# Cross attention and feed forward on one core: rows by DMA in the head, another order for q's third pair, and M and G in halves

## Chip, cores, metric

The kernel runs on one core of one Trainium2 chip. The metric is device time in microseconds of one execution; 16 blocks of the batch are worked off on that core.

## What is computed

The input x is (16, 128, 1024) and ctx is of the same shape; the middle dimension is the channel dimension of the attention (DIM 128), n runs over 1024 tokens, and there are 8 heads of 64. The reference, cut:

```
q: layernorm(x) over its last axis;  k = v = ctx
qh, kh, vh = Wq q, Wk k, Wv v            # (8 heads, 64, 1024)
qh = softmax(qh, over the 64) / 8;  kh = softmax(kh, over the 1024 tokens)
context = kh vh^T;  out = context^T qh;  out = Wo out + bo
x2 = x + out / max(norm(out over channels), 1e-12) * g * sqrt(128)
w = (4 bit weights from qweight, low and high nibble, minus round(zeros / scales)) * scales
result = x2 + layernorm(x2) w + bias
```

## The kernel before

One block is one index of the batch. The code writes a software pipeline of iterations i = -1 to 17, each of eight steps j = 0 to 7: iteration i prepares block n = i + 1 (load, normalise, split in high and low parts), does the projections of block a = i, the attention output of block c = i - 1 and the feed forward of block f = i - 2. Iterations 3 to 14 (on ACT to 12) are a hardware loop, the others are written out. Each engine runs its own instruction list in the order of the code; semaphores tie them together. There is no scheduler.

Per block: `project_q(j)` makes 128 tokens of q for all heads (three float32r products of high and low parts, into ps_q); DVE's `shift_q` takes off the maximum, ACT exponentiates, DVE's `sum_q` sums, GpSimd's `scale_q` normalises a pair of steps (pairs p = 0 to 3 are steps 2p and 2p + 1), ACT's `high_q` and GpSimd's `low_q` split the pair into two float16 tiles, and SP sends both through a transposing DMA (`turn_q`). `project_k(b, j)` makes 128 channels of k for all tokens (ps_k), DVE's `max_k` and ACT's `exp_k` work on it, PE transposes the result and ACT moves it to k_t. Since the context is linear in v, v is never projected: M = ctx^T k_exp (`mix_m`, eight full float32 products of 512 columns into ps_m, one for each 128 tokens), ACT moves it to m_t, and G = M^T vo for each head (`mix_g`, vo = Wv^T Wo^T made once in the head) goes to ps_o[0]. DVE's `split_g` scales G by k's sums into float16 g_hi and g_lo, in four column groups fc, and `mix_out(h)` gives the output for half h of the tokens, over the same four groups. ACT's `squares`, PE's column sums, GpSimd's rn and PE's spreads of rn give the norm; DVE's `attend` multiplies with it, GpSimd adds x_res to x2 and takes its rstd (`fit_x2`), ACT's `normalise_x2` writes x2n, and `feed_forward` multiplies with w_int.

In the head (iterations -1 to 1) the weights are transposed, vo is made, qweight's nibbles are cut out by DVE (`set_up_late`, eight steps into the tiles y and x_res in turn) and converted by ACT, and the rows scales, zeros / scales and bias / scales are spread over the partitions by PE transpositions into ps_o, copied by ACT (`set_up_ffn`), mixed and split into three bfloat16 parts in ffn_rows (`set_up_mix`, `set_up_split`).

The places that the change touches: mix_m L1168, called at steps 6 and 7 (L1376, L1391, L1395); mix_g L1185; split_g L881; move_m L596; gs_undo L879; on GpSimd fit_x2 at the start of the next iteration, scale_q(a, 2) at step 6, low_q(a, 2) at the end of step 7; on ACT high_q(a, 2) at step 6 and exp_k(a, s, 1) after high_q(c, 3).

## Time and profile before

| | us |
|---|---|
| median of 3 runs | 705.52 (703.21 to 708.35) |
| the profiled execution | 706.99 |
| its span, first to last instruction | 704.9 |
| PE, DVE, POOL, ACT busy | 654.4, 555.5, 474.5, 449.6 |
| mean granted TensorE clock | 0.978 |

The page tells busy times over the whole span; the queries behind it answer for a stretch, an engine or a line. PE is the matmul engine, PEld its weight loads, which overlap it, DVE is VectorE, ACT ScalarE, POOL GpSimd. Matmuls are pipelined, so the duration of one is longer than its share of the time; the distance between starts is what counts. "Idle before, released by" names what ended a wait, inferred from semaphores; where a wait is put down to "issue", the profile shows no releaser.

### The profile page before, as it was taken

The page shows a single profiled execution, that of the slowest core. Times are in us where ns is not written, and L with a number is a line of the kernel's source. Part 1 is how long each engine was busy: PE and PEld are TensorE (multiplying, and loading weights), DVE is VectorE, ACT ScalarE, POOL GpSimd, SP SyncE. Part 2 cuts the span into 40 slices and gives each one's busy share as a digit, 9 for nine tenths or more (in the row PEclk, how much of TensorE's full clock was granted, in tenths as well). Part 3 has the DMA queues.
Part 4 walks back from the last instruction along what each step waited for, and adds up shares of the span by engine and source line. Part 5 has one row for each costly group of instructions (what it writes and reads, how often), then busy time and mean ns, then how long its engine had stood idle before and what let it go on. Part 6 is the DMA issues. An engine that isn't in the chain of part 4 may idle for free.

```text
span 704.9 us, 11155 instructions
## 1 busy us (share of the span) xinstructions
PE 654.4 (93%) x3312; PEld 420.1 (60%) x3328; DVE 555.5 (79%) x900; ACT 449.6 (64%) x747; POOL 474.5 (67%) x406
## 2 busy tenths in 40 slices
PE   4858799999999999999999999999999999999987
PEld 3635556666666666656666666666666665666543
DVE  2997778888878788888878888888878887887844
ACT  3575666767585767667485666758575766748432
POOL 2166286776949496785949677694949678594820
PEclk9989889999999999999999999999999999999989
DMA  8125236363553637263454636255363724344451
GB/s 297 62 52 120 54 54 171 91 152 59 149 113 83 164 89 179 50 173 74 119 126 96 166 89 163 50 154 105 80 161 89 179 53 116 69 114 78 92 106 60
DMA packets 178871, 78.43 MB, mean 111 GB/s; under 512 B 168328, under 2 KB 169888, under 8 KB 178848
## 3 DMA queue, kind: packets, MB, share of 16 engines
q1 hardware_dynamic: 172512, 55.09, 36.9%
q10 hardware_dynamic: 6336, 23.07, 9.7%
q8 instruction: 10, 0.16, 0.1%
q14 instruction: 13, 0.11, 0.1%
HBM read 28.32 MB, written 8.39 MB: 52 GB/s over the span
## 4 chain that ended last, share of the span: by engine, by line
PE 34%; POOL 25%; issue 19%; DVE 12%; ACT 7%; DMA 1%; POOLq 0%; another core or an unknown queue 0%; DVEq 0%; ACTq 0%; SPq 0%
PE ps_m L1268 6%; POOL q_tok_lo L429 6%; POOL x L510 3%; POOL q_exp L419 3%; PE ps_m L1180 3%; POOL c_lo L473 3%; DVE q_sum L859 3%; POOL y L435 3%; PE ps_k L1110 3%; PE ps_o L1110 2%; POOL rn L492 2%; PE ps_k L1112 2%; PE ps_o L1111 2%; PE ps_k L1111 2%; PE ps_o L1112 2%
## 5 line engine op out<-in xcount | busy, mean ns | idle before, releaser
L429 POOL TENSOR_TENSOR q_tok_lo<-q_exp,q_tok_hi 128x1024 f16<-128x1024 f32 x64 | 140.0, 2189 | 85.8 <-ACT q_tok_hi L574 85.8
L419 POOL TENSOR_TENSOR q_exp<-q_exp,q_rec 128x1024 f32<-128x1024 f32 x64 | 122.2, 1910 | 5.0
L1180 PE MATMUL ps_m<-k_t,c_t 128*128 128x512 f32 x256 | 119.8, 602 | 0.0
L563 ACT ACTIVATE q_exp<-q_exp 128x512 f32<-128x512 f32 x128 | 80.5, 629 | 45.9 <-DVE q_exp L852 45.9
L840 DVE TENSOR_REDUCE k_nmax<-ps_k 128x1 f32<-128x1024 f32 x64 | 78.1, 1220 | 40.1 <-PE ps_k L1112 40.0
L558 ACT ACTIVATE k_exp<-ps_k,k_nmax 128x1024 f32<-128x1024 f32 x64 | 71.1, 1110 | 55.1 <-DVE k_nmax L840 55.1
L574 ACT ACTIVATE q_tok_hi<-q_exp 128x1024 f16<-128x1024 f32 x64 | 67.6, 1056 | 49.8 <-POOL q_exp L419 49.8
L847 DVE TENSOR_REDUCE q_nmax<-ps_q 128x8 f32<-128x512 f32 x128 | 87.3, 682 | 11.2 <-PE ps_q L1112 9.6
L852 DVE TENSOR_TENSOR q_exp<-ps_q,q_nmax 128x512 f32<-128x512 f32 x128 | 88.5, 692 | 5.1 <-DVE q_nmax L847 0.2
L1110 PE MATMUL ps_q<-wq_hi,xn_lo 128*128 128x512 f32 x128 | 74.4, 581 | 9.7 <-DVE q_exp L852 7.0
L417 POOL TENSOR_TENSOR q_rec<-q_rec,q_range 128x16 f32<-128x16 f32 x64 | 15.6, 244 | 93.3 <-DVE q_rec L862 93.3
L859 DVE TENSOR_REDUCE q_sum<-q_exp 128x16 f32<-128x1024 f32 x64 | 77.4, 1209 | 0.7 <-ACT q_exp L563 0.7
L1180 PEld LDWEIGHTS ps_m<-k_t,c_t 128*128 128x128 f32 x256 | 47.2, 194 | 41.6 <-issue 40.2
L1110 PE MATMUL ps_k<-c_hi,wk_lo 128*128 128x512 f32 x128 | 64.1, 501 | 8.2 <-ACT k_exp L558 8.1
L1110 PE MATMUL ps_o<-q_hi,g_lo 128*128 128x512 f16 x128 | 50.2, 392 | 9.3 <-issue 5.5
L1268 PE MATMUL ps_m<-w_int,x_hi 128*128 128x512 f16 x224 | 53.1, 380 | 0.0
L1268 PE MATMUL ps_m<-w_int,x_lo 128*128 128x512 f16 x224 | 52.9, 379 | 0.0
L1111 PE MATMUL ps_k<-c_lo,wk_hi 128*128 128x512 f32 x128 | 51.5, 403 | 0.0
L1112 PE MATMUL ps_k<-c_hi,wk_hi 128*128 128x512 f32 x128 | 51.5, 402 | 0.0
L1111 PE MATMUL ps_q<-wq_lo,xn_hi 128*128 128x512 f32 x128 | 51.2, 400 | 0.0
L1112 PE MATMUL ps_q<-wq_hi,xn_hi 128*128 128x512 f32 x128 | 51.0, 399 | 0.0
L1111 PE MATMUL ps_o<-q_lo,g_hi 128*128 128x512 f16 x128 | 50.2, 392 | 0.0
(185 smaller groups left out, 1385.1 us busy)
## 6 DMA issues: line engine op xcount, KB each, us to landing
x_res<-in_x ACTq DMA_DIRECT2D x16, 512.0 KB, 3.4
out_x<-y SPq DMA_DIRECT2D x15, 512.0 KB, 2.9
x_in<-in_x ACTq DMA_DIRECT2D x14, 512.0 KB, 4.7
c_in<-in_ctx ACTq DMA_DIRECT2D x14, 512.0 KB, 6.0
x_in<-in_x SPq DMA_DIRECT2D x2, 512.0 KB, 6.0
c_in<-in_ctx SPq DMA_DIRECT2D x2, 512.0 KB, 8.1
q_hi<-q_tok_hi SPq DMA_TRANSPOSE x64, 3.1
q_lo<-q_tok_lo SPq DMA_TRANSPOSE x64, 3.1
```

Source lines behind the costliest of these rows:

```text
L419: nc.gpsimd.tensor_tensor(pair, pair, rec.unsqueeze(2).to_broadcast([P, 2 * HEADS, DH]), ALU.mult).then_inc(qs_done, 1)
L429: nc.gpsimd.tensor_tensor(q_tok_lo[p % 2][:], q_exp[:, 2 * p:2 * p + 2, :].rearrange("p t d -> p (t d)"), q_tok_hi[p % 2][:], ALU.subtract ...
L563: nc.scalar.activation(q_exp[:, j, :], q_exp[:, j, :], ACT.Exp).then_inc(qexp_done, 1)
L840: nc.vector.tensor_reduce(k_nmax[:, j:j + 1], ps_k[:], op=ALU.max, axis=AX_X, negate=True).then_inc(kmax_done, 1)
L847: nc.vector.tensor_reduce(q_nmax[:, j, :], heads, op=ALU.max, axis=AX_X, negate=True).then_inc(qmax_done, 1)
L852: nc.vector.tensor_tensor(q_exp[:, j, :].rearrange("p (h d) -> p h d", h=HEADS), heads, q_nmax[:, j, :].unsqueeze(2).to_broadcast([P, HEAD ...
L859: nc.vector.tensor_reduce(q_sum[:, two, :], q_exp[:, two, :].rearrange("p t (h d) -> p t h d", h=HEADS), op=ALU.add, axis=AX_X).then_inc(q ...
L1110: nc.tensor.matmul(ps, lhs_lo, rhs_hi, start=start, stop=False)
L1111: nc.tensor.matmul(ps, lhs_hi, rhs_lo, start=False, stop=False)
L1112: return nc.tensor.matmul(ps, lhs_hi, rhs_hi, start=False, stop=stop)
L1180: last = nc.tensor.matmul(ps_m[:], c_t[s][:, t, :], k_t[:, t, :], start=(t == 0), stop=(t == TC - 1))
L1268: nc.tensor.matmul(ps_m[:], (x2_hi, x2_lo)[part][:, k, :], w, start=(part == 0 and k == 0), stop=False)
```

## The change

M is made in two groups of eight products with 256 columns (four heads) each: the first into ps_m at step 6, the second into ps_o[1] at the end of step 7, with G's first four heads between them. ACT moves the first half of M at step 6 of the same iteration and the second at the start of the next, where G's second half follows, into ps_m. DVE splits the first half of G at step 7 and the second after shift_q(0). The output product waits for the second half of G only at its third column group. On GpSimd scale_q(a, 2) goes behind the x2 addition and fit_x2 for the block's x2 goes ahead of low_q(a, 2); on ACT high_q of pair 2 moves to the start of the next iteration, and exp_k(1) ahead of high_q of pair 3. On DVE sum_q of pair 3 moves behind x2's statistics, and gs_undo becomes a tensor_scalar. In the head the scale row is broadcast by one DMA, the two other rows are split into three parts as 8 x 256 tiles and put into ffn_rows by 12 DMAs on SP's queue, after a memset of ffn_rows; four of the eight nibble steps move to iteration 1; vo is copied by ACT; x's statistics come first on DVE. Cut to its core:

```diff
+            sp.dma_start(scale_bc[:], scales.rearrange("o a -> (a o)").partition_broadcast(P)).then_inc(scale_spread, 16)
+            sp.wait_ge(consts_made, 10)
+            for part in range(3):
+                sp.wait_ge(rows_split, (1, 3, 4)[part])
+                for r in range(4):
+                    row = 32 * part + r
+                    sp.dma_start(ffn_rows[row:row + 1, :].rearrange("a (t c) -> a t c", t=TC),
+                                 row_parts[:, r // 3, part, :]).then_inc(rows_placed, 16)
...
+                first = isinstance(i, int) and i == FIRST
+                if first:
+                    fit_x()
+                    low_c()
...
-                    if j == 0 and do_f:
-                        fit_x2(f)
...
-                    if j == 6 and do_a:
+                    if j == 6 and isinstance(i, int) and i == END:
                         scale_q(a, 2)
...
+                    if j == 7 and do_a and not (isinstance(i, int) and i == END):
+                        scale_q(a, 2)
+                    if j == 7 and do_c and not (isinstance(i, int) and i == END):
+                        fit_x2(c)
...
+                    nc.scalar.activation(m_t[:, PART:], ps_o[1][:, 0:PART], ACT.Identity,
+                                         scale=g_fit[:]).then_inc(mb_moved, 1)
...
-                    if j == 4 and isinstance(i, int) and i == FIRST:
+                    if j == 4 and first:
+                        high_x()
                         set_up_rest()
+                    if j == 0 and isinstance(i, int) and i == 0:
+                        act.wait_ge(zero_steps, 5)
+                        nc.scalar.activation(row_parts[:, :, 0, :], rows_in[:, 1:3, :], ACT.Copy).then_inc(rows_split, 1)
                     if j == 0 and do_c:
                         move_m()
+                        high_q(c, 2)
...
+                    if j == 0 and do_a:
+                        exp_k(a, s, 1)
...
+                    if j == 6 and do_n and not first:
+                        high_x()
+                    if j == 6 and do_a:
+                        act.wait_ge(ma_ready, a + 1)
+                        if begun(a):
+                            act.wait_ge(ga_ready, a)
+                        act.wait_ge(fit_steps, 5 * a + 3)
+                        nc.scalar.activation(m_t[:, 0:PART], ps_m[:, 0:PART], ACT.Identity,
+                                             scale=g_fit[:]).then_inc(ma_moved, 1)
                     if j == 7 and isinstance(i, int) and i == END:
                         high_q(a, 2)
-                    if j == 6 and do_a and not (isinstance(i, int) and i == END):
-                        high_q(a, 2)
-                    if isinstance(i, int) and i == 0:
-                        set_up_ffn(j)
+                    if isinstance(i, int) and i == 0 and j == 0:
+                        move_vo()
                         act.wait_ge(rows_split, 2)
...
+                        nc.scalar.activation(row_parts[:, :, 1, :], rows_in[:, 1:3, :], ACT.Copy).then_inc(rows_split, 1)
+                    if isinstance(i, int) and i == 0 and j in (2, 4, 6, 7):
+                        convert_nibble((2, 4, 6, 7).index(j))
                     if isinstance(i, int) and i == 1 and j == 0:
-                        convert_nibble(2 * RC - 1)
-                        act.wait_ge(w_converted, 2 * RC)
                         nc.scalar.dma_start(x_res[:], x[c]).then_inc(xres_loaded, 16)
+                    if isinstance(i, int) and i == 1 and j in (2, 3, 4, 6):
+                        convert_nibble(4 + (2, 3, 4, 6).index(j))
...
-                    nc.vector.tensor_tensor(gs_undo[:], g_undo[:], gs_col[:], ALU.mult).then_inc(fit_steps, 1)
-
+                    if isinstance(i, int) and i == 0:
+                        dve.wait_ge(gs_done, 1)
+                    nc.vector.tensor_scalar(gs_undo[:], g_undo[:], gs_col[:], None, ALU.mult).then_inc(fit_steps, 1)
+
+                def split_g(b, part, chunks=(0, 1)):
+
+                    ps_g = (ps_o[0], ps_m)[part]
+                    two = slice(2 * part, 2 * part + 2)
+                    if 0 in chunks:
+                        if begun(2 * b):
+                            dve.wait_ge(out_ready, 2 * b)
+                        nc.vector.tensor_tensor(g_hi[:, two, :], ps_g[:, 0:PART].rearrange("p (c o) -> p c o", c=2),
+                                                k_rec[:, two].unsqueeze(2).to_broadcast([P, 2, P]),
+                                                ALU.mult).then_inc(ghi_done, 1)
+                        dve.wait_ge(ghi_done, 2 * b + part + 1)
+                    for k in chunks:
+                        fc = 2 * part + k
+                        nc.vector.scalar_tensor_tensor(out=g_lo[:, fc, :], in0=ps_g[:, k * P:(k + 1) * P],
                                                        scalar=k_rec[:, fc:fc + 1], in1=g_hi[:, fc, :],
                                                        op0=ALU.mult, op1=ALU.subtract).then_inc(glo_done, 1)
...
+                if isinstance(i, int) and i == FIRST:
+                    stats_x()
+                    mean_x()
+                    abs_c()
+                    norm_x()
+                    set_up()
                     set_up_rows()
+                    top_c()
+                    max_k(n, 0)
+                    return
...
                         sum_q(a, 2)
+                        dve.wait_ge(kexp_done, 4 * (a + 1))
+                        if begun(4 * a):
+                            dve.wait_ge(glo_done, 4 * a)
+                        nc.vector.reciprocal(k_rec[:], k_sum[:, s, :]).then_inc(krec_done, 1)
...
-                        set_up_split((j - 3) // 2)
+                        if j == 1:
+                            set_up_gains()
+                        elif j == 3:
+                            set_up_top()
+                        if j in (1, 3, 5, 6):
+                            pick_nibble((1, 3, 5, 6).index(j))
+                    if isinstance(i, int) and i == 1 and j in (1, 2, 3, 5):
+                        pick_nibble(4 + (1, 2, 3, 5).index(j))
...
                     if j == 7 and do_n:
                         max_k(n, 0)
-                    if j == 7 and do_a:
+                    if j == 7 and isinstance(i, int) and i == END:
                         sum_q(a, 3)
-                    if j == 7 and isinstance(i, int) and i == END:
                         for h in range(HALVES):
                             attend(c, h)
                             add_x(c, h, x2)
+                    if j == 7 and do_a:
+                        dve.wait_ge(ga_ready, a + 1)
+                        dve.wait_ge(krec_done, a + 1)
+                        split_g(a, 0, (0,))
                     if j == 7 and do_c:
...
                     if j == 7 and do_a:
-                        dve.wait_ge(kexp_done, 4 * (a + 1))
-                        nc.vector.reciprocal(k_rec[:], k_sum[:, s, :]).then_inc(krec_done, 1)
+                        split_g(a, 0, (1,))
                     if j == 7 and do_c:
                         nc.vector.bn_aggr(mv2[:], stats2[:].rearrange("p a b -> p (a b)")).then_inc(stats2_done, 1)
+                    if j == 7 and do_a and not (isinstance(i, int) and i == END):
+                        sum_q(a, 3)
...
-                def mix_m(t0, t1):
-
-                    if t0 == 0:
-                        pe.wait_ge(tk_moved, 8 * (a + 1))
-                        pe.wait_ge(tc_moved, 2 * (a + 1))
+                def mix_m(part):
+
+                    pe.wait_ge(tc_moved, 2 * (a + 1))
+                    if part == 0:
+                        pe.wait_ge(tk_moved, 8 * a + 4)
                         if isinstance(i, int) and i == 0:
                             pe.wait_ge(vtop_done, 1)
                         if do_c:
-                            pe.wait_ge(m_moved, c + 1)
+                            pe.wait_ge(glo_done, HC * (c + 1))
                         if do_f:
                             pe.wait_ge(ymul_done, 2 * (f + 1))
...
+                    else:
+                        pe.wait_ge(tk_moved, 8 * (a + 1))
+                        if isinstance(i, int) and i == 0:
+                            pe.wait_ge(vo_moved, 2)
+                        if do_n:
+                            pe.wait_ge(ctop_done, n + 1)
+                        if do_c:
+                            pe.wait_ge(att_done, 2 * (c + 1))
+                    cols_of = slice(part * PART, (part + 1) * PART)
+                    for t in range(TC):
+                        last = nc.tensor.matmul((ps_m, ps_o[1])[part][:, 0:PART], c_t[s][:, t, :], k_t[:, t, cols_of],
+                                                start=(t == 0), stop=(t == TC - 1))
+                    last.then_inc((ma_ready, mb_ready)[part], 1)
+
+                def mix_g(b, part):
+                    pe.wait_ge((ma_moved, mb_moved)[part], b + 1)
+                    if part == 0:
+                        if isinstance(i, int) and i == 0:
+                            pe.wait_ge(vo_moved, 2)
+                        if begun(2 * b):
+                            pe.wait_ge(att_done, 2 * b)
+                    for h in range(4 * part, 4 * part + 4):
                         rows = slice(DH * (h % 2), DH * (h % 2) + DH)
-                        last = nc.tensor.matmul(ps_o[0][rows, (h // 2) * P:(h // 2 + 1) * P],
+                        fc = h // 2 % 2
+                        last = nc.tensor.matmul((ps_o[0], ps_m)[part][rows, fc * P:(fc + 1) * P],
                                                 m_t[:, h * DH:(h + 1) * DH], vo[:, h * P:(h + 1) * P],
                                                 start=True, stop=True)
-                    last.then_inc(g_ready, 1)
+                    last.then_inc((ga_ready, gb_ready)[part], 1)
...
                     if h == 0:
-                        pe.wait_ge(ghi_done, c + 1)
-                        pe.wait_ge(glo_done, HC * (c + 1))
+                        pe.wait_ge(ghi_done, 2 * c + 1)
+                        pe.wait_ge(glo_done, HC * c + 2)
+                    else:
+                        pe.wait_ge(mb_moved, c + 1)
...
+                        if h == 0 and fc == 2:
+                            pe.wait_ge(ghi_done, 2 * (c + 1))
+                            pe.wait_ge(glo_done, HC * (c + 1))
...
-                        mix_m(0, 4)
+                        mix_m(0)
...
+                    if j == 7 and do_n and isinstance(i, int) and i == FIRST:
+                        project_k(n, 0)
                     if j == 7 and do_n:
                         transpose_c(1)
-                    if j == 7 and do_a:
-                        mix_m(4, 5)
-                    if j == 7 and do_n:
+                    if j == 7 and do_n and not (isinstance(i, int) and i == FIRST):
                         project_k(n, 0)
                     if j == 7 and do_a:
-                        mix_m(5, TC)
+                        mix_g(a, 0)
+                        mix_m(1)
```

On PE, in iteration 2 from the spreads of rn (into ps_o) to the iteration's end, before:

```order
L1384 MATMUL ps_o<-ident,rn 128x128 x8
L1142 MATMUL ps_tb<-ident,c_in 128x128 x4
L1180 MATMUL ps_m<-k_t,c_t 128x512
L1110 MATMUL ps_k<-c_hi,wk_lo 128x512
L1111 MATMUL ps_k<-c_lo,wk_hi 128x512
L1112 MATMUL ps_k<-c_hi,wk_hi 128x512
L1110 MATMUL ps_k<-c_hi,wk_lo 128x512
L1111 MATMUL ps_k<-c_lo,wk_hi 128x512
L1112 MATMUL ps_k<-c_hi,wk_hi 128x512
L1180 MATMUL ps_m<-k_t,c_t 128x512 x3
```

and now:

```order
L1433 MATMUL ps_o<-ident,rn 128x128 x8
L1181 MATMUL ps_tb<-ident,c_in 128x128 x4
L1149 MATMUL ps_k<-c_hi,wk_lo 128x512
L1150 MATMUL ps_k<-c_lo,wk_hi 128x512
L1151 MATMUL ps_k<-c_hi,wk_hi 128x512
L1149 MATMUL ps_k<-c_hi,wk_lo 128x512
L1150 MATMUL ps_k<-c_lo,wk_hi 128x512
L1151 MATMUL ps_k<-c_hi,wk_hi 128x512
L1242 MATMUL ps_o<-vo,m_t 64x128 x4
L1228 MATMUL ps_o<-k_t,c_t 128x256 x8
```

M's last four products of 512 columns are gone from there; eight of 256 columns stand at the end, G's first half ahead of them.

On GpSimd, in the same iteration from rn to its end, before (x2's rstd, `ve` to `nmr`, follows in the next iteration):

```order
L492 TENSOR_TENSOR rn<-n,neg_half 128x8
L417 TENSOR_TENSOR q_rec<-q_rec,q_range 128x16
L419 TENSOR_TENSOR q_exp<-q_exp,q_rec 128x1024
L499 TENSOR_TENSOR xn_lo<-xn,xn_hi 128x1024
L510 TENSOR_TENSOR x<-og,x_res 128x512 x2
L429 TENSOR_TENSOR q_tok_lo<-q_exp,q_tok_hi 128x1024
```

and now:

```order
L516 TENSOR_TENSOR rn<-n,neg_half 128x8
L523 TENSOR_TENSOR xn_lo<-xn,xn_hi 128x1024
L536 TENSOR_TENSOR x<-og,x_res 128x512 x2
L425 TENSOR_TENSOR q_rec<-q_rec,q_range 128x16
L427 TENSOR_TENSOR q_exp<-q_exp,q_rec 128x1024
L467 TENSOR_TENSOR ve<-mv,eps_col 128x1
L468 TENSOR_TENSOR nm<-mv,minus_col 128x1
L470 TENSOR_TENSOR rstd<-ve,neg_half 128x1
L472 TENSOR_TENSOR nmr<-nm,rstd 128x1
L454 TENSOR_TENSOR q_tok_lo<-q_exp,q_tok_hi 128x1024
```

The scaling of q's pair stands behind x2, and the four steps of x2's rstd ahead of q_tok_lo.

On DVE, from the second row of shift_q(7) in iteration 1 to the split of G in iteration 2, before:

```order
L852 TENSOR_TENSOR q_exp<-ps_q,q_nmax 128x512
L840 TENSOR_REDUCE k_nmax<-ps_k 128x1
L859 TENSOR_REDUCE q_sum<-q_exp 128x16
L862 RECIPROCAL q_rec<-q_sum 128x16
L1046 BN_STATS stats<-x 128x6 x2
L1050 RECIPROCAL k_rec<-k_sum 128x4
L1052 BN_AGGR mv<-stats 128x2
L847 TENSOR_REDUCE q_nmax<-ps_q 128x8
L852 TENSOR_TENSOR q_exp<-ps_q,q_nmax 128x512
L887 TENSOR_TENSOR g_hi<-ps_o,k_rec 128x512
L892 SCALAR_TENSOR_TENSOR g_lo<-ps_o,k_rec,g_hi 128x128 x4
```

and now (from max_k on):

```order
L858 TENSOR_REDUCE k_nmax<-ps_k 128x1
L908 TENSOR_TENSOR g_hi<-ps_o,k_rec 128x256
L914 SCALAR_TENSOR_TENSOR g_lo<-ps_o,k_rec,g_hi 128x128
L1105 BN_STATS stats<-x 128x6 x2
L914 SCALAR_TENSOR_TENSOR g_lo<-ps_o,k_rec,g_hi 128x128
L1110 BN_AGGR mv<-stats 128x2
L877 TENSOR_REDUCE q_sum<-q_exp 128x16
L880 RECIPROCAL q_rec<-q_sum 128x16
L865 TENSOR_REDUCE q_nmax<-ps_q 128x8
L870 TENSOR_TENSOR q_exp<-ps_q,q_nmax 128x512
L908 TENSOR_TENSOR g_hi<-ps_m,k_rec 128x256
L914 SCALAR_TENSOR_TENSOR g_lo<-ps_m,k_rec,g_hi 128x128 x2
```

The first half of G is split around the statistics of x2, sum_q comes behind them, and two g_lo instead of four stand behind shift_q(0).

## Rows read from the trace of the kernel before

**Rows 1.** page: the span, and busy us (share of it) xinstructions of each engine
```profile
span 704.9 us, 11155 instructions
PE 654.4 (93%) x3312; PEld 420.1 (60%) x3328; DVE 555.5 (79%) x900; ACT 449.6 (64%) x747; POOL 474.5 (67%) x406
```

**Rows 2.** waits, PE: who waited for whom, us in total, times, longest
```profile
PE ps_k L1110 <- ACT k_exp L558: 8.1, 11, 1.9
PE ps_o L1110 <- issue: 5.5, 8, 3.4
...
PE ps_o L1110 <- DVE g_lo L892: 3.8, 5, 0.8
```

**Rows 3.** stretches, blocks 0, 1, middle: length, busy PE, PEld, DVE, ACT, POOL, clock
```profile
21.15:63.12 41.97, 31.48 (x150) 21.48 (x149) 36.99 (x53) 28.16 (x45) 20.08 (x13) 0.89 0.22 50
63.12:109.24 46.12, 39.21 (x174) 25.93 (x176) 34.49 (x58) 29.62 (x43) 27.62 (x19) 0.85 0.39 81
...
390.17:430.30 40.13, 39.31 (x205) 25.31 (x206) 33.07 (x55) 26.92 (x45) 29.71 (x26) 1.00 0.47 117
```

**Rows 4.** timeline, PE, two neighbouring blocks: start, us, instruction [idle before]
```profile
356.94 0.50 PE L1110 MATMUL ps_k<-c_hi,wk_lo 128*128 128x512 f32 x1 [0.60 <-ACT k_exp L558]
...
393.02 0.60 PE L1164 MATMUL ps_tb<-ident,k_exp 128*128 128x128 f32 x4
394.37 0.38 PE L1110 MATMUL ps_o<-q_hi,g_lo 128*128 128x512 f16 x1 [0.75 <-DVE g_lo L892]
...
397.14 0.50 PE L1110 MATMUL ps_k<-c_hi,wk_lo 128*128 128x512 f32 x1
```

**Rows 5.** chain that ended last, in order of time: start, us, what
```profile
456.61 1.68 PE ps_o L1367 x16
...
458.89 3.44 PE ps_m L1180 x8
462.33 0.23 PE ps_q L1110
```

**Rows 6.** line L1180 (M): its weight loads, duration ns min/median/max
```profile
L1180 PEld LDWEIGHTS ps_m<-k_t,c_t x256: 187/190/337, 49.4 to 666.8; 128*128 128x128 f32 x128
```

**Rows 7.** timeline, DVE, the split of G in a middle block
```profile
392.07 0.68 DVE L887 TENSOR_TENSOR g_hi<-ps_o,k_rec 128x512 f16<-128x512 f32 x1
392.78 1.13 DVE L892 SCALAR_TENSOR_TENSOR g_lo<-ps_o,k_rec,g_hi 128x128 f16<-128x128 f32 x4
```

**Rows 8.** timeline, POOL, then ACT, around that block's start
```profile
382.24 1.90 POOL L419 TENSOR_TENSOR q_exp<-q_exp,q_rec 128x1024 f32<-128x1024 f32 x1
...
386.45 2.50 POOL L510 TENSOR_TENSOR x<-og,x_res 128x512 f32<-128x512 f32 x2
388.92 2.13 POOL L429 TENSOR_TENSOR q_tok_lo<-q_exp,q_tok_hi 128x1024 f16<-128x1024 f32 x1
...
391.92 0.19 POOL L447 TENSOR_TENSOR nmr<-nm,rstd 128x1 f32<-128x1 f32 x1
...
392.15 1.34 ACT L638 ACTIVATE og<-x,nmr,rstd 128x1024 f32<-128x1024 f32 x1 [2.59 <-POOL nmr L447]
```

**Rows 9.** timeline, DVE: g_undo; and line L879, duration ns min/median/max
```profile
415.17 0.15 DVE L877 TENSOR_SCALAR g_undo<-g_unit 128x1 f32<-128x1 f32 x1
...
L879 DVE TENSOR_TENSOR gs_undo<-g_undo,gs_col x16: 621/1143/2135, 49.0 to 655.3; 128x1 f32<-128x1 f32 x16
```

**Rows 10.** timeline, the head: xn_lo, and first and last late nibble step
```profile
17.42 2.34 POOL L499 TENSOR_TENSOR xn_lo<-xn,xn_hi 128x1024 fp32r<-128x1024 f32 x1 [2.02 <-ACT xn_hi L744]
...
43.54 2.18 DVE L830 TENSOR_SCALAR y<-og 128x1024 int32<-128x1024 int32 x1 [0.51 <-ACT w_int L535]
...
59.83 0.80 DVE L830 TENSOR_SCALAR x_res<-x 128x1024 int32<-128x1024 int32 x1 [2.51 <-ACT w_int L535]
```

**Rows 11.** groups by line, DVE, 20 to 97 us: xcount | busy, mean ns
```profile
L804 DVE TENSOR_TENSOR bias_bc<-zero_bc,ffn_rows 128x1024 f32<-128x1024 f32 x1 | 1.2, 1215 | 0.0
```

**Rows 12.** timeline, PE, the last block's first product of out
```profile
673.14 0.59 PE L1110 MATMUL ps_o<-q_hi,g_lo 128*128 128x512 f16 x1 [3.42 <-issue]
```

283 lines of the change are left out of this document (112 added, 171 removed).

## Prediction

> **What bounds the kernel now.** Four views were read. The page first: the matmul engine is busy 93% of the 704.9 us span, and next come DVE with 79% and GpSimd with 67% [rows 1]. The stretch view says where that holds: in the middle one block takes 40.13 us, with 39.31 us of PE work in it; block 0 takes 41.97 us and block 1 46.12 us although they lack the feed forward part, and there DVE (36.99 us busy of 41.97) or nobody (block 1, DVE 34.49 of 46.12) is full, and the granted clock is 0.89 and 0.85 [rows 3]. So there are two programs: a steady one bound by PE with small holes, and a head bound by latencies, with DVE as its fullest engine.
>
> The view of who waited for whom names the steady holes: ps_k waits 8.1 us in 11 places for k's exponential, ps_o 3.8 us for g_lo and 5.5 us for "issue", which at this place is the same group of waits [rows 2]. In order of time they are two places in a block: the first product of out, 0.75 us, and project_k of part 2, 0.60 us in the block before it [rows 4]. With the gaps that carry no name (the transposition that starts at 393.02 is through 0.44 us later, the product starts at 394.37) I take 1.2 us a block.
>
> **Part 1, M and G in halves, steady blocks.** M is 8 products of 512 columns; each goes as two passes, and 8 passes take 3.44 us, 0.43 each [rows 5]. After it there are 16 products of 256 columns, the same columns, but twice the weight loads: 16 more passes a block. If a short pass is half a long one, 32 x 0.215 = 6.88 us, as before. The load of such weights shows 190 ns [rows 6], less than 215, so I take it as hidden, and the sum has +0.05 us. The bound above: a float32r pass has the same load and streams for the same time as a short pass would, and it costs 0.23 us [rows 5]; 32 x (0.234 - 0.215) = +0.6 us a block. The bound below is 0: the columns are the same. G's 8 products stay, in two groups of four, with one more change of operands: +0.1 us.
>
> What goes: today g_hi (0.68) and four g_lo (1.13) stand between G and the first product of out [rows 7]. After it the first half of G is split in the block before, and the second half costs DVE half of this, 0.9 us, and PE asks for it only at the third of four column groups, about 1.3 us after it starts. PE has project_k, a transposition, project_q and a transposition (2.3 us) between the second half of G and that start. The hole is gone. M's second half is moved by ACT (0.69 us for 512 columns now, about 0.4 for 256) under project_q and project_k of the next block, 1.4 us; the first half's move lies under the rn spreads, project_k(n, 0) and more. New waits: the second half of M goes to ps_o[1] and waits for both attend products; DVE starts them when the rn spreads are there and needs 1.3 us, and PE has a transposition (0.44), project_k (1.4) and half of G (0.5) first: 1 us to spare.
>
> **Part 2, the third pair of q.** On GpSimd today the order is scaling of q's pair 2, xn_lo, x2 (2.50), q_tok_lo (2.13), then x2's rstd, whose last step starts at 391.92; ACT's normalisation waits 2.59 us for it [rows 8]. Behind that wait in ACT's queue stand exp_q(0), x2n_hi, q_tok_hi of pair 3 and then k_exp(1), for which PE waits. After it x2 comes 2.1 us earlier, and rstd before q_tok_lo. By hand from the same rows: xn_lo to 384.7, x2 to 387.2, scaling (1.90) to 389.3, rstd ready at 390.4 instead of 392.1. ACT then does M's half, q_tok_hi of pair 2 (1.06, moved here from before the block's end) and its three DMA starts and gets to the normalisation at 392.0, no wait left; k_exp(1) no longer stands behind q_tok_hi of pair 3 (1.06 us) and ends at about 395.9, when PE, now 1 us earlier, wants it at 396.1. Hidden, with 0.2 us to spare. q_tok_lo of pair 2 comes 2 us later (393.0), its transposition leaves SP just ahead of x2_hi's, and pair 2 is wanted only by the second half of out, 15 us later. SP's order is the same.
>
> **Part 3, DVE.** gs_undo takes 1143 ns in the median for one column, its neighbour of the other form 0.15 [rows 9]; as tensor_scalar it gives back 1.0 us a block, in front of scale_y, off PE's path. But in the stretch from attend to the second half of G DVE now has, in a row, attend 1.3, shift_q 1.4, max_k 1.2, half of G's split 1.0, statistics 1.4, sum_q 1.45, shift_q(0) 1.4: 9.15 us from 383.2 give 392.35, and PE wants shift_q(0)'s end at about that time, for project_q(1). I put 0.25 us of new waiting there. Steady sum: -1.2 + 0.25 + 0.1 = -0.85 us a block, 14 times (blocks 2 to 15): **-11.9**.
>
> **Part 4, the head.** Start: xn_lo starts at 17.42 after a wait of 2.02 us for xn_hi [rows 10]; x's statistics go first now, which makes xn about 3 us earlier, but c_lo and project_k (to 17.3) then bound project_q(0) instead, at 18.2 for 19.9: **-1.5**. The memset of ffn_rows lies under PE's wait for its first weights. Block 0: the DVE work of 36.99 us loses vo's two copies (1.3, to ACT, whose six row copies of 0.6 go), four of eight nibble steps (43.54 to 59.83: 2.18, two of 0.7, 0.80) with waits of 0.51 and 2.51 us for ACT [rows 10], gs_undo's 2.0; it gains 0.9 of G's split. That is -6.8 of work and -3.0 of waits; what comes instead are latencies of the k chain, which PE, DVE and ACT go through in turn, so I take two thirds: **-7**. Block 1: DVE loses the mixing and splitting of rows, about 4.5 us (one of them 1.2 [rows 11]) and 0.8 of gs_undo, gains four nibble steps (2.9); its wait of 2.0 us for G goes, as does the path through ACT's ffn_rows copies, which four nibble copies replace. It had 11.6 us idle: **-4.5**, bounds 0 and -8. The row DMAs: 12 small ones and one broadcast on SP, ahead of q's first transposition; their data are wanted by block 0's feed forward, two iterations later. Hidden; if SP were late with them, q's turns would slip, but out wants these only in block 1.
>
> **Part 5, the tail.** The first product of out waits 3.42 us [rows 12], and with G's first half done early that wait goes. But M's second half now waits for attend's second product, which in the last block stands behind an x2 addition, so most of the wait moves there: **-1**.
>
> Sum: -1.5 - 7 - 4.5 - 11.9 - 1 = -25.9 against the profiled run's 707.0 (704.9 span and 2.1 around it): 681.1. The median run is 1.5 below the profiled one: **680 us**.
>
> **Rivals.** (a) The short pass costs what a float32r pass costs: +0.6 x 16 = +9.6, 689.5. For it: both have the same load and stream about as long. Against: in the long float32 pass (0.43 us, two cycles a column at 2.4 GHz) nothing is added, so the 20 ns may belong to float32r's own stream. (b) The slower side: loads are not hidden behind short passes. 256 more loads in the kernel: at 0.105 us, the pace of ps_o with one column a load (16 in 1.68 [rows 5]), +27, 707; at 190 ns +49, 728. It decides from 25.9 / 256 = 0.10 us a load. Against it: the long passes at 0.43 show nothing of their loads. The Trainium skill speaks for it: TensorE: Matmul & The Clock Gate, section The mechanism (packing small matmuls), states that a weight load overlaps a running matmul only when the row groups differ, and here all are full height. By that rule today's M would show its loads too; the trace disagrees, since 8 passes in 3.44 us are 1032 cycles each at 2.4 GHz, all but 8 of them the stream. (c) The steady block stays at 40.2 because DVE or GpSimd now ends last (their new order makes shift_q(0) late by as much as the holes gave): 680 + 12 = 692. For it: the 9.15 us row of DVE above has no slack. Against: DVE is busy 33.07 of 40.13 [rows 3]. (d) The head gives twice: block 0 to 31, block 1 to 37: about 672.
>
> **How the numbers follow.** Forecast with its own range 675 to 686: 0.45; (a) 0.20; (b) 0.06; (c) 0.13; (d) 0.12; 0.04 for other things. From 669 to 694 all but (b) and the rest are in. Three runs of this kernel lie within 0.7%, so 1% (7 us) is about what can be told from no change: faster by over 1%, below 698.5, is everything but (b) and half of the rest, 0.92; within 1%: (b) at its low price and a little, 0.05; slower 0.03.
>
> **What would show it.** In the profile after: a steady block of 39.2 to 39.5 us; M's two groups at 3.44 us for 16 passes (3.7 if (a), over 5 if (b)); no wait of ps_o for g_lo, at most 0.3 us of ps_q for DVE's q_exp in a block; ACT's normalisation without its 2.6 us wait; gs_undo at 0.2 us; block 0 at 33 to 36 us, block 1 at 39 to 43. A block over 39.9 with short passes at 0.215 would say that (c) holds. What would make it wrong above all: the price of a short pass, and the head, where I add up work of one engine where three take turns.

## The result and the profile after

The changed kernel is slower: median 722.4 us (719.2 to 728.7, four runs) against 704.7 us of the kernel before on the same chip, ratio 1.025, 95% interval 1.017 to 1.033. I had forecast 680. The profiled execution has a span of 717.5 us, 12.6 more than before, and PE's share fell from 93% [rows 1] to 92%, though it now executes more instructions:

```profile
span 717.5 us, 11719 instructions
PE 658.9 (92%) x3541; PEld 469.0 (65%) x3557; DVE 553.2 (77%) x909; ACT 447.7 (62%) x757; POOL 473.2 (66%) x409
...
PE 62%; DMA 8%; POOL 8%; DVE 7%; SPq 5%; issue 5%; ACT 4%; another core or an unknown queue 0%; ACTq 0%; POOLq 0%; DVEq 0%
```

The last line is the chain that ended last: DMA has 8% of it and SyncE's queue (SPq) 5%. To place the loss, both spans are cut at two events that they share: the first product of project_q(0) in block 2, and M's first product in the last block. Their rows, before (L1110, L1180) and after (L1149, L1228), in the timelines of PE:

```profile
60.18 0.48 PE L1110 MATMUL ps_q<-wq_hi,xn_lo 128*128 128x512 f32 x1 [0.27 <-issue]
...
107.21 0.80 PE L1110 MATMUL ps_q<-wq_hi,xn_lo 128*128 128x512 f32 x1
...
659.94 3.60 PE L1180 MATMUL ps_m<-k_t,c_t 128*128 128x512 f32 x8
```

```profile
16.88 0.58 PE L1149 MATMUL ps_q<-wq_hi,xn_lo 128*128 128x512 f32 x1
...
54.05 0.59 PE L1149 MATMUL ps_q<-wq_hi,xn_lo 128*128 128x512 f32 x1
...
95.20 0.58 PE L1149 MATMUL ps_q<-wq_hi,xn_lo 128*128 128x512 f32 x1
```

In the changed kernel M's last group starts at 670.63. So the head is 12.0 us shorter (107.21 to 95.20), the middle 22.7 longer (552.7 to 575.4), the tail 1.9 longer (45.0 to 46.9). The stretch view of the middle, first before, then after (length, then busy PE, PEld, DVE, ACT, POOL, then the granted clock, DMA share and GB/s):

```profile
107.21:659.94 552.73, 540.91 (x2805) 349.30 (x2818) 453.38 (x744) 371.15 (x624) 407.56 (x343) 1.00 0.49 114
```

```profile
95.20:670.63 575.43, 550.02 (x3006) 391.17 (x3018) 455.97 (x752) 374.51 (x636) 406.57 (x342) 0.99 0.51 110
```

PE was idle 11.8 us of the middle before and 25.4 after. The view of who waited for whom has one name for nearly all of it:

```profile
PE ps_m L1321 <- DMA x_hi<-x2n_hi: 23.5, 11, 5.6
```

The small holes for which the change was made are nearly gone (25.4 - 23.5 = 1.9 us are left of 11.8). In their place the feed forward waits in 11 blocks for x_hi, the transposed upper half of the normalised x2. One block in order of time, first PE, then ScalarE's copy, then the queues of SyncE and ScalarE (start, duration, for the queues that of the issue, instruction):

```profile
404.36 0.23 PE L1273 MATMUL ps_o<-ident,rs_parts 128*128 128x128 bf16 x1
407.86 1.90 PE L1321 MATMUL ps_m<-w_int,x_hi 128*128 128x512 f16 x8 [3.27 <-DMA x_hi<-x2n_hi]
...
398.32 1.04 ACT L680 ACTIVATE x2n_hi<-og 128x1024 f16<-128x1024 f32 x1
...
395.76 1.23 SPq L354 DMA_TRANSPOSE q_hi<-q_tok_hi  x1
398.08 2.17 SPq L354 DMA_TRANSPOSE q_lo<-q_tok_lo  x1
400.35 5.43 SPq L379 DMA_TRANSPOSE x_hi<-x2n_hi  x1
...
394.89 0.34 ACTq L731 DMA_DIRECT2D x_res<-in_x  x1
395.49 0.34 ACTq L734 DMA_DIRECT2D x_in<-in_x  x1
396.07 0.34 ACTq L738 DMA_DIRECT2D c_in<-in_ctx  x1
```

x2n_hi is ready in time (ACT's copy runs from 398.32 to 399.36). What is slow is the transposing DMA: its issue alone takes 5.43 us. In the same block before, q_hi's transposition of pair 2 was issued at 385.40, 3.7 us ahead of the first of the three loads, q_lo's at 391.08, behind all three, and x_hi's at 395.07 with an issue of 1.23 us:

```profile
385.40 1.23 SPq L347 DMA_TRANSPOSE q_hi<-q_tok_hi  x1
391.08 1.23 SPq L347 DMA_TRANSPOSE q_lo<-q_tok_lo  x1
395.07 1.23 SPq L372 DMA_TRANSPOSE x_hi<-x2n_hi  x1
...
389.12 0.34 ACTq L693 DMA_DIRECT2D x_res<-in_x  x1
389.71 0.34 ACTq L696 DMA_DIRECT2D x_in<-in_x  x1
390.29 0.34 ACTq L700 DMA_DIRECT2D c_in<-in_ctx  x1
```

The waits also cost clock. Behind three of the five waits of 3 us and more, PE runs its first products at the lower of its two levels (1.2 for 2.4 GHz): after the wait of 4.6 us the six us from 321.65 have a granted clock of 0.50. The whole stretch 321.65 to 364.78 has 0.93 and 42.49 us of PE work, its neighbour at 1.00 has 39.63.

```profile
321.65:364.78 43.13, 42.49 (x219) 29.74 (x221) 31.72 (x53) 25.24 (x41) 27.69 (x23) 0.93 0.45 109
364.78:407.86 43.08, 39.63 (x220) 28.41 (x221) 34.73 (x58) 28.96 (x52) 30.81 (x27) 1.00 0.56 111
```

### The profile page after: what moved, and what is told of

It is laid out like the page before. It is cut to its first block, busy times and chain, and to the rows that moved or that the text cites. A ratio compares the mean times of both kernels' runs of the same rounds, so it can differ in the third digit from the quotient of the medians.

```text
span 717.5 us, 11719 instructions
## 1 busy us (share of the span) xinstructions
PE 658.9 (92%) x3541; PEld 469.0 (65%) x3557; DVE 553.2 (77%) x909; ACT 447.7 (62%) x757; POOL 473.2 (66%) x409
## 4 chain that ended last, share of the span: by engine, by line
PE 62%; DMA 8%; POOL 8%; DVE 7%; SPq 5%; issue 5%; ACT 4%; another core or an unknown queue 0%; ACTq 0%; POOLq 0%; DVEq 0%
PE ps_m L1321 13%; DMA x_hi<-x2n_hi 8%; PE ps_o L1228 7%; PE ps_m L1228 7%; SPq L354 4%; POOL q_tok_lo L454 4%; PE ps_o L1416 3%; PE ps_q L1149 3%; PE ps_q L1150 3%; PE ps_q L1151 2%; PE ps_k L1149 2%; PE ps_k L1150 2%; PE ps_ta L1203 2%; PE ps_k L1151 2%; PE ps_o L1149 2%
## 5 line engine op out<-in xcount | busy, mean ns | idle before, releaser
L454 POOL TENSOR_TENSOR q_tok_lo<-q_exp,q_tok_hi 128x1024 f16<-128x1024 f32 x64 | 138.5, 2164 | 123.7 <-ACT q_tok_hi L607 123.7
L1321 PE MATMUL ps_m<-w_int,x_hi 128*128 128x512 f16 x224 | 57.9, 405 | 23.5 <-DMA x_hi<-x2n_hi 23.5
L1149 PE MATMUL ps_q<-wq_hi,xn_lo 128*128 128x512 f32 x128 | 68.5, 535 | 3.9 <-DVE q_exp L870 3.9
L1149 PE MATMUL ps_k<-c_hi,wk_lo 128*128 128x512 f32 x128 | 61.2, 478 | 2.7 <-ACT k_exp L582 2.7
L1228 PE MATMUL ps_o<-k_t,c_t 128*128 128x256 f32 x256 | 61.8, 396 | 0.0
L1228 PE MATMUL ps_m<-k_t,c_t 128*128 128x256 f32 x256 | 59.3, 386 | 0.0
L1228 PEld LDWEIGHTS ps_o<-k_t,c_t 128*128 128x128 f32 x256 | 49.0, 196 | 9.3 <-issue 2.9
L1321 PEld LDWEIGHTS ps_m<-w_int,x_hi 128*128 128x128 f16 x224 | 20.6, 102 | 51.2 <-DMA x_hi<-x2n_hi 25.0
L1228 PEld LDWEIGHTS ps_m<-k_t,c_t 128*128 128x128 f32 x256 | 48.7, 195 | 6.3
```

Source lines behind the costliest of these rows:

```text
L454: nc.gpsimd.tensor_tensor(q_tok_lo[p % 2][:], q_exp[:, 2 * p:2 * p + 2, :].rearrange("p t d -> p (t d)"), q_tok_hi[p % 2][:], ALU.subtract ...
L1149: nc.tensor.matmul(ps, lhs_lo, rhs_hi, start=start, stop=False)
L1228: last = nc.tensor.matmul((ps_m, ps_o[1])[part][:, 0:PART], c_t[s][:, t, :], k_t[:, t, cols_of], start=(t == 0), stop=(t == TC - 1))
L1321: nc.tensor.matmul(ps_m[:], (x2_hi, x2_lo)[part][:, k, :], w, start=(part == 0 and k == 0), stop=False)
```

## The experiments

Theory: ScalarE's three bulk loads (x_res, x_in, c_in, 512 KB each) and the transpositions of q's third pair, which the change brought into the same few us, delay x_hi's transposition. Rivals: the place in SyncE's queue, x2's chain, and M and G in halves. Each ratio is that to the kernel before as measured with the run, its 95% interval in brackets; "wait" is the sum for PE ps_m <- DMA x_hi.

### The loads moved, the queue swapped, the pair undone, the pair alone

```
# e1: ScalarE, the three loads
-  if j == 0 ...: nc.scalar.dma_start(x_res ...), (x_in ...), (c_in ...)
+  if j == 3 ...: the same
```

> The changed kernel, with ScalarE's three bulk loads (x_res, x_in, c_in, 512 KB each) started at step 3 instead of step 0, so in a stretch without transposing DMAs. Theory: in the changed kernel x_hi's transposing DMA waits because 1.5 MB of loads and the transpositions of q's third pair are drained by the same 16 DMA engines in the same 10 us. The issue of x_hi then takes 1.3 us in every block instead of up to 7.4, the wait of ps_m for x_hi falls from 23.5 us to under 2, no half-speed stretch of TensorE's clock is left in the middle, and the time is 688 to 694 us. Rival: it is the place in SyncE's queue alone (x_hi stands right behind q_lo of pair 2): then nothing changes, 715 to 725 us, and x_hi's issue still takes 4 to 7 us in half of the blocks. Second rival: the wait is x2's chain (rstd, normalisation, x2n_hi) being late: then the wait stays too, with short issues.

694.4 us (693.4 to 695.4), ratio 0.986 [0.984, 0.988]. x_hi's issue (minimum, median, maximum in ns) is short in every block, and the wait is gone:

```profile
L379 SPq DMA_TRANSPOSE x_hi<-x2n_hi x14: 1277/1289/1328, 102.3 to 623.4; - x14
```

The theory holds in mechanism and, at the upper end of its range, in time. But a block takes 40.2 us, as before: PE now waits 0.4 to 0.6 us for k_t, which ScalarE moves behind the three DMA starts.

```
# e2: SyncE, blocks 1 to 14
-  turn_q(a, 2, "hi"); turn_q(a, 2, "lo")      # then x2_hi
+  turn_q(a, 2, "hi")                          # then x2_hi, then turn_q(c, 2, "lo")
```

> The changed kernel, with SyncE's order alone changed: x_hi's transposing DMA ahead of q_lo's of pair 2 in blocks 1 to 14. Theory (shared DMA engines): x_hi has one transposition less ahead of it, by 1.8 us of engine time, but the loads and q_hi of pair 2 stay: the wait of ps_m for x_hi goes from 23.5 us to 0 to 8 us, 693 to 705 us. Rival (place in the queue alone): the wait is gone, 688 to 692 us. Rival (the loads alone, no transposition needed): x_hi's issue still takes 4 us or more in half of the blocks, 710 us or more.

715.4 us (712.9 to 718.7): worse than both of my numbers for theory and queue rival, and nearest the rival of the loads. The wait is 16.7 us in 6 places, x_hi's issue 1.99 us in the median and 3.58 at most; what it no longer bears, q_lo's issue bears behind it (up to 6.8 us). So the place in the queue is not the cause, and one transposition less ahead of x_hi is not the cure.

```
# e3: the pair at its old place
+  if j == 6 and do_a: scale_q(a, 2)   # GpSimd;  ScalarE: high_q(a, 2) at j == 6
-  if j == 7 ...: scale_q(a, 2)        # GpSimd;  ScalarE: high_q(c, 2) at next j == 0
```

> The changed kernel with q's third pair back at its old place (scaled on GpSimd and copied on ScalarE at step 6, ahead of x2), x2's rstd still ahead of q_tok_lo, M and G in halves and the head as changed. Theory: q_hi and q_lo of pair 2 leave SyncE 5 to 7 us before x_hi again, the wait for x_hi goes, but k_exp(1) or x2's rstd may be late by 0.5 us a block: 690 to 698 us. Rival (M and G in halves, not the pair, make x_hi late): 715 us or more.

694.1 us (693.7 to 694.6): with the pair back the wait is gone, the halves stay and do no harm to x_hi. A new wait of ps_q for q_exp of 0.6 us stands in every second block.

e4 puts the same part alone into the kernel before (its diff is part 2 of the change).

> The kernel before with this part alone: q's third pair scaled and copied behind x2, x2's rstd ahead of q_tok_lo, k_exp(1) ahead of q_tok_hi of pair 3; M whole, head as before. Theory: x_hi's issue is stalled here too (4 us and more in about half of the blocks), and ps_m waits 15 to 30 us for x_hi in all: 715 to 735 us. Rival (the stall needs M and G in halves as well, or the faster head): 700 to 708 us.

752.1 us (749.5 to 754.3), ratio 1.067 [1.064, 1.071]. The direction is the theory's, the size beyond my range: one part alone costs 48 us, since here nearly every block has the long issue.

```profile
L372 SPq DMA_TRANSPOSE x_hi<-x2n_hi x13: 1262/5037/7212, 111.0 to 644.2; - x13
...
PE ps_m L1271 <- DMA x_hi<-x2n_hi: 37.8, 11, 7.1
```

c_in's load lands after 10.5 us in the median, for 6.0 before.

### A better place for the loads, the tail, and the bytes

```
# e5: ScalarE;  e7: the same in e4
   if j == 4 and do_c: squares(0); squares(1)
+  if j == 4 ...: the three loads
   if j == 4 and do_a: high_q(a, 1)
```

> The changed kernel with the three bulk loads started behind the squares and og copies of step 4, where ScalarE waits 1.6 us for GpSimd anyway and the 16 DMA engines are nearly idle for the next 15 us. In the run with the loads at step 3 a block took 40.2 us with 0.5 us of waiting for k_t behind the three DMA starts on ScalarE. Theory (that wait is the price of the DMA starts on ScalarE's queue, and without it the block is bound by 39.6 us of PE work): blocks of 39.7 to 39.8 us, 686 to 689 us. Rival (another chain, DVE's with shift_q, takes over): a wait of 0.3 to 0.6 us of ps_q for q_exp and blocks of 40.0 to 40.2 us: 692 to 695 us.

688.5 us (688.2 to 690.4), ratio 0.978 [0.974, 0.981], as the theory has it. Two blocks take 79.37 us with 79.18 of PE work:

```profile
299.34:378.71 79.37, 79.18 (x442) 56.78 (x441) 67.28 (x111) 54.34 (x93) 59.69 (x51) 1.00 0.49 119
```

> As e4_before_pair2 (752 us: the kernel before with q's third pair behind x2), with the three bulk loads started behind the squares of step 4. Theory (the 48 us are a collision of loads and transpositions): x_hi's issue is 1.3 us in every block again and the time is 696 to 704 us. Rival (part of the 48 us is the order of x2 and q themselves): above 710 us.

700.1 us (698.2 to 701.2), ratio 0.993 [0.990, 0.995]: moving three DMA starts takes 52 us from e4, all of its loss of 48 and a little more. e9 tells that the new place is worth nothing by itself:

> The kernel before, with nothing changed but the place of the three bulk loads: behind the squares of step 4, as in e5. Theory: there was no collision in the kernel before, only the 1.7 us of DMA starts on ScalarE ahead of the normalisation and k_exp(1): 0.1 to 0.3 us a block, 700 to 704 us. Rival (the loads' place costs nothing as long as nothing collides): 704 to 706 us. With it the worth of q's third pair behind x2 is e7's 700.1 us against this.

705.7 us against 705.6, ratio 1.000 [0.999, 1.002]: the rival. The kernel before had no collision, and the pair's part is worth 5.7 us (e7 against e9) once it has none either.

```
# e6: e5, DVE, last block, j == 7
+  attend(c, 0); attend(c, 1)
   sum_q(a, 3)
-  attend(c, 0); add_x(c, 0); attend(c, 1); add_x(c, 1)
+  add_x(c, 0); add_x(c, 1)
```

> As e5_loads_behind_squares, and in the last block's step 7 DVE's two attend products stand ahead of sum_q(3), the x2 additions behind it. Theory: the 5.3 us in which PE waits for attend ahead of G's first half fall to under 1.5 us, and M's second half no longer runs at half speed; x2's transposition may come later than its feed forward part by 1 to 2 us: 3 to 5 us less than e5. Rival (the tail is bound by x2's and q's chains, and the wait only moves to the first products of out or to the feed forward): within 1 us of e5.

687.7 us (687.4 to 689.7): the rival. The wait for attend falls from 5.3 to 1.0 us, but later in the same tail PE waits 3.7 us for the last transposition of q_lo instead:

```profile
657.61 0.38 PE L1151 MATMUL ps_o<-q_hi,g_lo 128*128 128x512 f16 x1 [3.68 <-DMA q_lo<-q_tok_lo]
```

```
# e8: the changed kernel, the loop's loads of left halves only
-  x_res[:] <- x[c];  x_in[s][:] <- x[i + 2];  c_in[s][:] <- ctx[i + 2]
+  the same, columns 0 to 511 of both sides
```

> The changed kernel with the loop's loads of x_res, x_in and c_in cut to their left 512 columns, 256 KB each, at their place of step 0 (the right halves keep the first blocks' values, so this part of the work is left out). Theory: half the bytes are drained by the time x_hi is asked for; its issue is under 2 us in most blocks and the wait for it under 6 us in all: 690 to 700 us. Rival (it is the presence of loads, or the order on SyncE's queue, not their bytes): the wait stays above 15 us, 710 to 722 us.

The right halves keep the first blocks' values, so this kernel leaves out a part of the work. 690.1 us (688.9 to 692.6), wait 0.5 us. With half the bytes the stall fits under other work, yet it is not gone: x_hi's issue takes 2.3 to 3.6 us in every second block up to 458 us, 1.26 in the others. The blocks alternate, with the same bytes in each. That speaks against bytes as the whole story.

### The order of a load and a transposition

The changed kernel shows the same alternation, and it goes with one thing. In the block above (long issue, wait 3.3 us) q_hi's transposition at 395.76 precedes c_in's load by 0.31 us. In the next block, with a wait of 0.8 us, it precedes it by 0.06:

```profile
438.25 0.34 ACTq L734 DMA_DIRECT2D x_in<-in_x  x1
438.82 0.36 ACTq L738 DMA_DIRECT2D c_in<-in_ctx  x1
...
438.76 1.28 SPq L354 DMA_TRANSPOSE q_hi<-q_tok_hi  x1
441.08 4.08 SPq L354 DMA_TRANSPOSE q_lo<-q_tok_lo  x1
445.25 1.26 SPq L379 DMA_TRANSPOSE x_hi<-x2n_hi  x1
```

It is the same in the ten blocks from 141 to 530 us: 0.35, 0.30, 0.31, 0.31 and 0.30 us ahead where the wait is 3.0 to 5.6 us, 0.03 to 0.06 where it is 0.4 to 1.3. c_in's load shows it too: it lands after 9.7 to 12.5 us in the five slow blocks and after 6.2 to 6.8 in the five quick ones. Quick doesn't mean undisturbed: there q_lo's issue takes 3.7 to 4.4 us, as above, but little of the wait is left behind it. In the slow blocks q_lo's takes 2.2 to 2.7 and x_hi's 4.9 to 7.4. The buffers of x_in and c_in alternate from block to block as well; they alone are not the cause, since in e4 the long issue stands in ten blocks one after the other, with c_in's load 0.16 to 0.31 us behind q_hi's transposition in each.

```
# e10: ScalarE, step 0
-  move_m(); high_q(c, 2); the three loads; normalise_x2()
+  move_m(); the three loads; high_q(c, 2); normalise_x2()
```

> The changed kernel, with ScalarE's three loads started ahead of q_tok_hi of pair 2 instead of behind it, so that all three stand in the rings before q_hi's transposition is issued; bytes and transpositions as changed. In the changed kernel the blocks with long waits (3 to 5.6 us) are those in which c_in's load starts 0.3 us after q_hi's transposition, those with 0.5 to 1.3 us have it starting 0.04 to 0.06 us after it or earlier. Theory (a bulk load started behind a transposition is what is slow): no block with a wait over 1 us, 688 to 695 us. Rival (only the sum of bytes and transpositions in those 10 us counts): waits of 15 us and more in all remain, 705 to 720 us.

709.0 us (705.9 to 710.0). The mechanism is the theory's, the time is not: x_hi's issue is 1.26 to 1.30 us in every block and PE never waits for it, but a block takes 41.2 us, because q_tok_hi, the normalisation, k_exp(1) and k_t all come later on ScalarE (PE waits 0.6 us for k_t and 0.3 for rs_parts, and more is lost in small steps that have no name). I had left that cost out.

```
# e11: ScalarE, step 0
-  move_m(); high_q(c, 2); the three loads; normalise_x2()
+  move_m(); high_q(c, 2); normalise_x2(); the three loads
```

> The changed kernel, with the three loads started 2 us later, behind the normalisation of x2, so that q_hi's transposition of pair 2 (and in part q_lo's) is issued before all of them. Theory (a load behind a transposition is slow): every block has the long wait, c_in lands 9 us and more after its start, 730 to 760 us. Rival (the sum alone counts): as the changed kernel or a little worse, 715 to 730 us.

752.7 us (751.0 to 755.6), as the theory has it, wait 45.3 us in 12 blocks; c_in starts 0.5 to 1.0 us behind q_hi's transposition and lands after 9.7 us in the median.

```profile
L379 SPq DMA_TRANSPOSE x_hi<-x2n_hi x14: 1289/5950/8507, 102.1 to 684.4; - x14
  PE ps_m L1321: 45.3, 12
```

e10 and e11 moved the loads in time too. e13 moves nothing on ScalarE.

```
# e13: SyncE, blocks 1 to 14
+  sp.wait_ge(xres_loaded, 16 * (a + 1))
   turn_q(a, 2, "hi"); turn_q(a, 2, "lo")
```

> The changed kernel, with one wait added on SyncE: q_hi's transposition of pair 2 is not issued before x_res's load of the same step has landed (3.4 us after its start), so that all three loads stand in the rings ahead of every transposition, in all blocks, at the changed kernel's own times. Theory (order): c_in lands within 7 us in every block, x_hi's issue takes under 1.5 us, the wait of ps_m for x_hi is 0 to 0.6 us a block, 690 to 697 us. Rival (sum in the window): the same bytes and transpositions are squeezed into less time ahead of x_hi: waits of 20 us and more in all, 715 us or more.

692.9 us (692.2 to 693.2), ratio 0.984 [0.981, 0.986], 29.5 us less than the changed kernel by holding two transpositions back. They are now issued back to back with x_hi's, in 2.7 us for 4.6 in the slow block above (timeline of both queues):

```profile
258.96 0.34 ACTq L740 DMA_DIRECT2D c_in<-in_ctx  x1
...
261.72 1.23 SPq L354 DMA_TRANSPOSE q_hi<-q_tok_hi  x1
263.05 1.26 SPq L354 DMA_TRANSPOSE q_lo<-q_tok_lo  x1
264.40 1.51 SPq L379 DMA_TRANSPOSE x_hi<-x2n_hi  x1
```

Who waited for x_hi in this run (us in all, times):

```profile
  PE ps_m L1323: 2.5, 5
```

c_in lands after 5.7 us in the median. The longest wait is 1.2 us, for 0.6 expected; the rest is as the theory has it, and the rival's 715 us are out: the same bytes and the same three transpositions don't cost 30 us by themselves. That the order alone decides is not shown, though. Here c_in's load starts 2.1 to 2.8 us ahead of q_hi's transposition and, in the block shown, 5.4 us ahead of x_hi's (4.3 in the slow block), and x_res's load has landed. e10 gives the loads a head start of 1.6 to 1.7 us as well. And e5 has the order that should be slow: its loads start behind q_lo's transposition of another pair, which lands 5.1 us after its own start, and no transposition follows for 3.8 us:

```profile
354.56 1.23 SPq L354 DMA_TRANSPOSE q_lo<-q_tok_lo  x1
355.23 0.34 ACTq L766 DMA_DIRECT2D x_res<-in_x  x1
356.33 0.34 ACTq L773 DMA_DIRECT2D c_in<-in_ctx  x1
360.14 1.23 SPq L354 DMA_TRANSPOSE q_hi<-q_tok_hi  x1
```

There c_in lands after 5.7 us (5.7 to 7.4 over the run), and q_hi's issue is short. So a load behind one transposition isn't slow as such; in the slow block above two more transpositions are issued 2.0 and 4.3 us behind c_in's start.

```
# e14: c_in's load alone behind the squares, x_res and x_in at step 0
```

> The changed kernel, with c_in's load alone moved behind the squares of step 4; x_res and x_in stay at step 0, started ahead of q_hi's transposition in every block. Theory (order): no long wait is left, all blocks alike, 689 to 693 us. Rival (sum in the window): as with loads of half the size, issues of x_hi of 2 to 3.6 us in alternate blocks and waits under 5 us in all, 690 to 697 us; if c_in's load has nothing to do with it, 715 us or more.

689.4 us (688.2 to 691.5), no wait for x_hi, issue at most 1.39 us: as the theory has it.

### M whole, and the pair with it

e12 is e5 with mix_m, mix_g, move_m and split_g of the kernel before.

> As e5_loads_behind_squares (688.5 us), with M whole again (8 products of 512 columns in ps_m, moved at once) and G whole at step 0, its split on DVE in one piece: the head and q's pair as changed. Theory: the halves take away a wait of 0.4 us a block for g_lo and cost 0.15 to 0.3 us a block in G and its changes of operand, so that they are worth 3 to 5 us in the blocks and lose 1 to 2 in the tail: 689 to 693 us here. Rival (the halves were worth what I forecast, 0.9 us a block less 0.1): 698 us or more; if they are worth nothing: 688 us.

686.1 us (685.4 to 687.6; a fourth execution, which took 2322 us, is left out), ratio 0.974 [0.972, 0.976] against e5's 0.978 [0.974, 0.981]. My own range (689 to 693) is missed: the halves are worth nothing that the intervals could tell. The middle of both, M whole first:

```profile
96.09:640.53 544.44, 538.39 (x2819) 350.12 (x2818) 449.39 (x743) 374.70 (x625) 408.34 (x343) 1.00 0.49 117
```

```profile
95.10:640.11 545.01, 543.49 (x3019) 388.49 (x3018) 460.85 (x752) 375.21 (x636) 407.47 (x343) 1.00 0.49 117
```

The halves take 4.5 us of holes away (6.05 to 1.52) and add 5.1 us of work (538.4 to 543.5).

e15 is e12 with the pair at its old place (e3's edit).

> As e12_whole_m (686.9 us: M and G whole, loads behind the squares), with q's third pair back at its old place ahead of x2 on GpSimd and at step 6 on ScalarE; x2's rstd stays ahead of q_tok_lo and k_exp(1) ahead of q_tok_hi of pair 3. Theory (the block's last hole is g_lo's 0.8 us in every second block, and x2's chain had slack once rstd goes first): 686 to 689 us, the moved pair is worth nothing. Rival (x2 2 us later makes the normalisation and k_exp(1) late again): a wait of ps_k for k_exp of 0.3 to 0.6 us a block, 691 to 696 us.

701.8 us (699.7 to 702.3): both my numbers are too low, and the wait is another one than the rival's. x2 comes 2 us later, and on DVE its statistics now stand ahead of sum_q(3) and shift_q(0), another part of the change:

```profile
419.53 0.69 DVE L1083 BATCH_NORM_STATS2 stats<-x 128x6 f32<-128x512 f32 x1 [0.53 <-POOL x L533]
420.70 0.69 DVE L1083 BATCH_NORM_STATS2 stats<-x 128x6 f32<-128x512 f32 x1 [0.48 <-POOL x L533]
```

PE waits 0.4 to 0.9 us for q_exp in each block, and 0.8 us for g_lo in twelve blocks instead of five (9.2 us for 3.8 in e12); a block takes 40.8 us. The pair's new place is worth 15 us in this company. That it is DVE's new order which needs it is read from these rows; no run changed that order by itself.

## Why the prediction was wrong

**The step that failed** is in part 2: "its transposition leaves SP just ahead of x2_hi's, and pair 2 is wanted only by the second half of out, 15 us later. SP's order is the same." I asked who wants q_lo, not what q_hi's and q_lo's transpositions do to the transfers around them. The order in SP's queue is the same; the starts in SP's queue against those in ScalarE's are not. The transpositions of the pair came in among the three loads, x_hi's own issue rose from 1.23 us to as much as 7.4, and PE waited 23.5 us for it in 11 blocks. The three DMA starts stood in part 2's list and had no price but their time on ScalarE. No rival had this: (c) is the nearest, and it named DVE and GpSimd. The sign that I had set for it, a block over 39.9 us with short passes at 0.215, came true in most blocks (up to 46.9 us) and would have pointed at the wrong engine. The rest of part 2 came as forecast: ACT's normalisation waited 36.9 us for nmr in the middle before and doesn't wait for it now, and ps_k's waits for k_exp fell from 8.1 us in 11 places to 2.7 in 3.

**The size.** In the middle, 22.7 us are 23.5 of waiting for x_hi, minus 9.9 of other holes (11.8 to 1.9), plus 9.1 of PE work. Of these 9.1, 2.6 are there in e5 at full clock as well (543.5 against 540.9), and the other 6.5 I put down to products at the lower clock. Without 23.5 and 6.5 the span of 717.5 would be 687.5; e5, which has neither, has 686.8: head -12.1, middle -7.7, tail +1.7, together -18.1 where I had forecast -25.9. So even without the collision 7.8 us of the forecast are missing.

**Part 1** had the short pass right: 16 of them go in 3.27 us from the first start to the next product's (382.95 to 386.22), and rivals (a) and (b) are out. The Trainium skill (TensorE: Matmul & The Clock Gate, The mechanism) says in its list of what overlaps that a weight load overlaps a running matmul only where the row groups differ. That is not borne out here: loads of 190 ns under passes of 0.215 us leave no trace. The same section's opening, which also lets loads into a background buffer go ahead, would fit. But the sum "+0.05" and "+0.1" was too small. The work of halves is 5.1 us in the middle, 0.37 a block: G takes 0.58 and 0.59 us in two groups for 1.02 in one, one more change of operand form stands ahead of it, and the second group of M takes 3.37 us. And the hole of "1.2 us a block" was 0.85 by the stretch view (11.8 us over 13.8 blocks); I had probably taken pipeline time between groups for idle time.

**Part 3.** DVE's wait of 0.25 us is not there in e5 (PE is idle 0.1 us a block). gs_undo is at 0.21 us, as forecast. Steady sum: -0.85 forecast, -0.5 without the collision (39.7 for 40.2 us).

**Part 4, the head**: -12.0 for -13. The parts are less good than the sum: the start gives 3.0 (1.5 forecast), block 0 3.1 (7), block 1 5.9 (4.5), by project_q(0)'s starts 19.90, 60.18 and 107.21 before and 16.88, 54.05 and 95.20 after. The row DMAs are hidden.

**Part 5, the tail**: +1.9 for -1. I had M's second half wait for attend; it is G's first half already, which needs both attend products of the block before to be done with ps_o. Both stand behind sum_q(3), the second behind an x2 addition of 2.15 us too, PE is idle 5.3 us, and M's second half, at the lower clock, then takes 6.00 us for the usual 3.7:

```profile
680.38 1.12 PE L1242 MATMUL ps_o<-vo,m_t 128*64 128x128 f32 x8 [5.26 <-DVE og L929]
681.43 6.00 PE L1228 MATMUL ps_o<-k_t,c_t 128*128 128x256 f32 x16
```

e6 shows that q's last transposition is next.

**The bound of the range.** The rivals reached from 672 to 728, but the high end hung on a cause that the trace all but excluded. The chance of slower, 0.03, was far too low for a change that shifts DMA starts of one queue against those of another.

## What to carry to other kernels

When an edit moves the producer of a DMA, write down all queues' DMA starts around its new place, with both orders, before calling it hidden: here two transpositions, unwanted for 15 us, moved in among three bulk loads and cost some 30 us, and one semaphore wait (29.5 us) or another place for the loads (33.9 us) gave it back. A hole filled by cutting work finer must be charged with the finer work: 4.5 us of holes were bought for 5.1 us of PE time. The best version here is the changed one with the loads behind the squares and M whole: 686.1 us, 2.6% faster than before.
